# Graph layer with linear attention and routed experts on one core: expert 16's load, the low halves, the edge groups' register read, and 92 edge groups instead of 69

## What is computed

```
xn  = layernorm(x)
agg = segment_sum(xn[src], dst, 1250)              # the edges
g   = xn + relu(bn(relu(bn(((1+eps)*xn + agg) @ W1 + b1)) @ W2 + b2))
q, k = elu(xn@Wq+bq)+1, elu(xn@Wk+bk)+1 ; v = xn@Wv+bv
m   = (q (k^T v)) / (q . sum k)  per head, @ Wp + bp   # linear attention
x   = x + g + m
x   = x + experts(layernorm(x))                    # 64 experts, two per token, hash routed
```

## Time and profile before

| | us |
|---|---|
| three runs | 548.93, 550.38, 551.34 (median 550.38) |
| the profiled execution, whole | 551.58 |
| its span, first to last instruction | 549.8 |
| busy in the span: PE, DVE, ACT, POOL | 529.9, 347.8, 253.7, 90.7 |
| rows, K and edges | 9.65 to 101.9 |
| Q and edges | 101.9 to 144.8 |
| aggregation | 145.2 to 204.6 |
| dense layers and router | to 366 (their last products start at 365.9) |
| routing and first gather | 366 to 382.6 |
| 32 rounds of experts | 382.6 to 531.5 |
| the late rounds' scatter by products, output | to the end |

### The profile page before, as it was taken

How to read it: one execution, slowest core, us unless ns; L and a number is a source line. 1 busy time by engine, 2 the same in 40 slices (tenths; PEclk the granted TensorE clock), 3 DMA queues, 4 the chain that set the end, 5 groups by cost and what they waited for, 6 DMA issues and landing times.

```text
span 549.8 us, 8615 instructions
## 1 busy us (share of the span) xinstructions
PE 529.9 (96%) x2857; PEld 369.3 (67%) x2858; DVE 347.8 (63%) x985; ACT 253.7 (46%) x557; POOL 90.7 (16%) x119
## 2 busy tenths in 40 slices
PE   9899999999989999999999999996999999999997
PEld 7344444554579888799999999984545545555445
DVE  6978797777875556448886233497435534453777
ACT  4878487666445443046664211456343334333300
POOL 2304012000000000000000000004244444445310
PEclk9999999999999999999999999999899999999999
DMA  8500000000100009192008223986999999999968
GB/s 313 204 2 1 2 0 2 1 0 2 61 17 1 0 3 335 48 352 99 0 1 344 77 77 98 413 331 233 389 407 414 418 415 410 415 416 417 393 263 317
DMA packets 32426, 105.70 MB, mean 192 GB/s; under 512 B 4656, under 2 KB 10033, under 8 KB 25340
## 3 DMA queue, kind: packets, MB, share of 16 engines
q1 hardware_dynamic: 23852, 88.54, 41.5%
q0 software_dynamic: 4880, 9.78, 4.7%
q10 hardware_dynamic: 3648, 6.80, 3.4%
HBM read 93.48 MB, written 17.84 MB: 202 GB/s over the span
## 4 chain that ended last, share of the span: by engine, by line
PE 73%; DMA 9%; DVE 6%; issue 6%; ACT 2%; POOL 2%; DVEq 1%; ACTq 0%; POOLq 0%
PE PS L538 8%; PE PS L537 8%; PE PS L539 8%; PE PS L626 6%; DMA BIG<-xx_rows,TIDX 5%; PE PS L853 5%; PE PS L589 4%; PE PS L655 4%; PE PS L867 4%; PE PS L578 4%; PE PS L656 4%; PE PS L772 3%; DMA XG<-xx_rows,TIDX 3%; PE PS L615 3%; PE PS L549 2%
## 5 line engine op out<-in xcount | busy, mean ns | idle before, releaser
L537 PE MATMUL PS<-ROUND 128*128 128x416 f32 (+3 forms) x232 | 83.9, 361 | 0.0
L538 PE MATMUL PS<-ROUND 128*128 128x416 f32 (+3 forms) x232 | 83.6, 360 | 0.0
L539 PE MATMUL PS<-ROUND 128*128 128x416 f32 (+3 forms) x232 | 83.4, 359 | 0.0
L867 PE MATMUL PS<-BIG 128*64 128x512 f32 x208 | 52.9, 593 | 0.2 <-issue 0.2
L1107 DVE BATCH_NORM_STATS2 BST<-BIG 128x6 f32<-128x416 f32 (+1 forms) x36 | 20.6, 590 | 44.0 <-ACT BIG L1471 35.4
L655 PE MATMUL PS<-ROUND 128*128 128x416 f32 (+3 forms) x120 | 43.5, 363 | 2.3 <-DVE ROUND L1024 1.8
L537 PEld LDWEIGHTS PS<-ROUND 128*128 128x128 f32 (+1 forms) x232 | 43.5, 188 | 2.6
L539 PEld LDWEIGHTS PS<-ROUND 128*128 128x128 f32 (+1 forms) x232 | 43.6, 188 | 2.5
L538 PEld LDWEIGHTS PS<-ROUND 128*128 128x128 f32 (+1 forms) x232 | 43.5, 188 | 2.4
L1006 DVE TENSOR_TENSOR BIG<-PS,BIG 128x280 f32 (+17 forms) x69 | 30.6, 444 | 19.8 <-PE PS L615 16.1
L987 DVE TENSOR_SCALAR BIG<-BIG 128x180 f16<-128x180 f16 (+20 forms) x157 | 42.2, 317 | 0.0
(11 more groups left out here) (275 smaller groups left out, 974.4 us busy)
## 6 DMA issues: line engine op xcount, KB each, us to landing
BIG<-in_we SPq DMA_DIRECT2D x46, 1024.0 KB
BIG<-in_we SPq DMA_DIRECT2D x12, 512.0 KB
y_rows<-KVB SPq DMA_DIRECT2D x19, 256.0 KB
BIG<-y_rows SPq DMA_DIRECT2D x9, 512.0 KB, 8.3
EXTRA<-in_we SPq DMA_DIRECT2D x4, 1024.0 KB
XA<-in_we SPq DMA_DIRECT2D x4, 1024.0 KB
BIG<-in_wqkvp SPq DMA_DIRECT2D x3, 1024.0 KB, 10.8
XA<-in_we SPq DMA_DIRECT2D x6, 512.0 KB
```

The source lines that it names most:

```text
L537: mm(o, ah, bh, start=first, stop=False)
L538: mm(o, ah, bl, start=False, stop=False)
L539: return mm(o, al, bh, start=False, stop=last)
L867: ins = mm(PS[64 * j:64 * j + 64, b, :], HT[:, s, 128 * f2 + 64 * j:128 * f2 + 64 * j + 64], weights(2 * r + j, 1024 + 512 * f2, 512), sta ...
```

## The change

Five edits:

1. The hand-written cost in `edge_groups` counts more for a tile and for its width. The best cut has 92 groups instead of 69: of one tile 43 (6 before), of two 38 (46), of three 6 (9), of four 5 (8). `front_schedule` spreads them over the same due times as before.
2. The step `"xl"` of row tile i is due at `done + 3.4 + 2.7*i`: one in each of the first ten units of Q's products, instead of in the aggregation.
3. The register read moves from the step `"ata"` to the step `"oh"` of the same group, ahead of its one-hots, with the wait for `LOROW`.
4. `LOROW` lies in a spare part of `XG4`.
5. SyncE issues the load of expert 16 after the waits for tiles 0 to 7, ahead of the wait for tiles 8 and 9.

```diff
-            work = m * (33 + w) + 2 * (16 + w) + (best[t + m])
+            work = m * (36 + 1.6 * w) + 2 * (16 + w) + (best[t + m])
...
             if c == 0:
-                at(base + turn * i - 1.7, "xl", i)
+                at(done + 3.4 + 2.7 * i, "xl", i)
...
-        LOROW = sb("LOROW", [1, NG], I32)
+        LOROW = XG4[0:1, 418:418 + NG].bitcast(I32)
...
                     if g == 0:
                         dve.wait_ge(s_key, NKEY["key"])
                         dve.wait_ge(s_oh, 1)
+                        dve.wait_ge(sd_low, 32)
                     if g >= OHG:
                         b, use = at_of(("at", g - OHG))
                         dve.wait_ge(full[b], use)
+                    first[g] = dve.value_load(LOROW[0:1, g:g + 1], min_val=0, max_val=N - w)
...
                     g, (b, use) = step[1], at_of(("at", step[1]))
-                    if g == 0:
-                        dve.wait_ge(sd_low, 32)
                     w = GRP[g][2]
-                    first = dve.value_load(LOROW[0:1, g:g + 1], min_val=0, max_val=N - w)
...
-                    win = AT16[:, :, bass.ds(first, w)]
+                    win = AT16[:, :, bass.ds(first.pop(g), w)]
...
             for q, (i, e) in enumerate(GROUPS):
+                if q == 2:
+                    load_expert(16)
                 sp.wait_ge(sd_xx[q], 16 * (e - i))
-            load_expert(16)
             sp.wait_ge(sd_xg[1], 16)
```

More of the change, by code:

```diff
@@ L902, in link @@
                 dve.wait_ge(s_link, done[0])
+            first = {}
             KBIi, SMIi = KBI.bitcast(I32), ORD.bitcast(I32)
```

## The result

| | before | after |
|---|---|---|
| median of 10 runs each, us | 550.60 (548.93 to 552.79) | 553.24 (551.97 to 554.55) |
| ratio to before | | 1.0046, interval 1.0027 to 1.0065 |
| the profiled execution, whole / its span | 551.58 / 549.8 | 554.55 / 552.7 |
| Q's first and last product | 102.1, 144.2 | 107.3, 151.6 |
| aggregation's last product | 204.7 | 209.3 |

The change makes the kernel 2.6 us slower; 546.7 had been forecast, with 551.5 as the upper end. The loss stands complete at Q's first product (5.2 us late), grows to 7.4 at Q's last, and comes back in part: 2.8 us in the aggregation and 1.0 from the router to the first transposes.

What follows compares the result with a forecast made beforehand. The front was taken to go at TensorE's pace; -3.1 - 0.4 - 1.8 + 1.5 + 0.4 + 0 - 0.3 = -3.7 us gave 546.7 us from the 550.38 median, with an 8-in-10 range of 543.0 to 551.5.

Steps and rivals of the forecast that it cites:

- Part 1: TensorE in the front: narrower groups save 7,520 columns, -3.1 us (1.3 before Q, 1.8 in Q).
- Part 4: VectorE in Q's first nine units: 95% full, TensorE waits, +1.5 us; later reciprocals, +0.4 us.
- Part 3: Aggregation: moving low halves removes TensorE's waits, -0.4 us at its first product and -1.8 us at row tile 8.
- Part 5: VectorE's register reads: exposure and removed waits taken as equal before Q, 0 (-1.5 to +2.3 us).
- point of decision: Exposed read time for a group at which cost equals the gains, 0.21 us; above it the change loses.
- part 2: VectorE in the front: 23 more but narrower additions, 2.8 us spread over it; VectorE gets no lighter.
- the five waits that the forecast added up: TensorE's waits for VectorE's window addition in the profile before, together 3.1 us.
- Part 6: Start of the experts: expert 16's load issued 1.1 us sooner, first gather sees less of it, -0.3 us.
- The collision with the last two writes: Rival, chance 0.08: expert 16's load delays the last writes, gather up to 1.0 us later, 0.3 lost: 548.0.
- The first round at full clock: Rival, chance 0.07: a shorter wait keeps the experts' first-round clock up, gaining 1.8 us and some 0.5: 544.4.
- the reads' rival: Rival, chance 0.20: reads show and VectorE bounds Q; +8.0 us against 5.6 of gains, 552.8.
- L615's waits above 6 us: Sign in TensorE's waits for the window addition: a sum above 6 us means the reads' rival is right.

Runs made afterwards that it cites:

- e7: Kernel before with only the low halves moved into Q's units and expert 16's load issued earlier: 547.18 us, ratio 0.9943.
- e9: Changed kernel with tiles 107 to 114 in four pairs (88 groups) and the register read left at the addition: 544.63 us, ratio 0.9892.
- e12: Changed kernel (92 groups) with the register read left at the addition: 550.75 us, ratio 1.0002.
- e11: e7 with tiles 107 to 114 cut single (73 groups) and LOROW in its new place: 551.26 us, ratio 1.0012.
- e8: Changed kernel with tiles 107 to 114 in four pairs instead of eight single tiles (88 groups): 548.31 us, ratio 0.9960.
- e2: Kernel before with only the ten low halves moved among Q's products: 547.28 us, ratio 0.9945.
- e13: e12 with GpSimd's last addition of K's features waiting for the product of the fifth one-tile group: 550.45 us, ratio 1.0001.
- e5: Changed kernel with the register read behind its group's one-hots instead of ahead of them: 551.68 us, ratio 1.0028.
- e10: e8 with the register read behind its group's one-hots instead of ahead of them: 545.45 us, ratio 0.9904.
- e1: Kernel before with only expert 16's load issued ahead of the wait for the last two writes: 549.55 us, ratio 0.9984.
- e3: Kernel before with only the finer cut (92 groups) and LOROW's new place, read at the addition: 552.95 us, ratio 1.0041.
- e4: Kernel before (69 groups) with only the register read moved ahead of the one-hots and LOROW's new place: 553.21 us, ratio 1.0049.
- e14: e9 with GpSimd's last addition of K's features behind the product of the third pair: 544.91 us, ratio 0.9899.
- e6: Changed kernel with the old cut of 69 groups, read ahead of the one-hots: 547.86 us, ratio 0.9955.

## Why the forecast failed, step by step

From before to after in four steps, each kernel against its own before: edits 2 and 5 -3.0 (e7), 88 groups without the run -3.4 (e9), the run +6.1 (e12), the read moved ahead of the one-hots +2.9 (after): +2.6. Worked out from the intervals of the ratios, each of the last three steps is known to about 1.6 us either side, and the first to 1.1; e11 against e7 (+3.3) shows the run, and e8 against e9 (+4.5) the read, a second time.

**Part 1, columns: right, and they arrive.** Without the run 6,360 columns are saved, by the forecast's 0.42 ns 2.7 us; e9 is 3.4 faster than e7, each against its own before (2.6 between the medians). Before Q this cut saves 1,960 columns, 0.8 us by the same pitch; Q's first product came 1.3 sooner in the traces (100.2 for 101.5). In Q the forecast had 1.8 of gain, 1.5 of loss and 0.4 at the reciprocal, +0.1; measured from first to last product 41.7 (100.2 to 141.9) for e7's 42.3, -0.6.

**Part 4, VectorE in Q: right in size, the 1.5 too careful.** Busy time was forecast at about 29 and is 28.7 in e9, 29.6 in after. At 94% TensorE still runs full. The wait behind the first reciprocal rises from 0.67 us before to 1.19 in e9 and 1.30 in after, near the forecast's +0.4.

**Part 3, low halves: right.** -0.4 and -1.8 forecast, -0.8 and -2.0 in e2's trace. The wait of 1.78 us of the earlier trace rows is gone, and nothing else took its place.

**Part 5, reads taken at 0: the first step that failed.** They cost 2.9 us with the run (after against e12) and 4.5 without (e8 against e9). At Q's first product it is 2.0 (102.2 for 100.2), within the bound of 2.3 but at its bad end; in Q 43.6 us for 41.7, 1.9 more. What was set against it, the waits that the read had caused at 40 and 44, was not worth that: e8 has 5.0 us of TensorE's waits for the addition, nine of them, and e9 2.5 in four. The error was in weighing the read at the addition and the read at the one-hots as equal. At the addition VectorE mostly waits for TensorE anyway (in e9 8.3 of the 12.6 us of idle time there end by TensorE, 2.9 by "issue"), and the read lies inside that wait; at the one-hots nothing is waited for, so it pushes the one-hots, and with them the next product, later. The rival for this had the right place and sign, and its 552.8 is near 553.2, but not its price: with 0.29 us exposed at 21 groups in Q and at 8 before it came to 8.0, and it was 4.5 at most. In after VectorE's "issue" time ahead of one-hots is 12.0 us over 92 groups, an average of 0.13, below the 0.21 at which the forecast had set its point of decision; and e8, with the read moved and no run, is 1.9 faster than before. So the reads alone don't make the change a loss, and the rival's sum met the measured time by luck: something else, the next point, was missing from it.

**Not in the forecast at all: the run of one-tile groups.** Part 1 summed columns over stretches, and part 2 spread the 23 additions over the front. The cut doesn't spread them. One list position has five groups with nothing between them, and two banks let only two products go ahead of the additions. There a group costs a round trip of about 0.9 us and not its 0.08 us of columns. This is 6.1 us (e12 against e9), 3.3 in the old cut (e11 against e7), 4.5 with the read ahead (after against e8). The trace of before had the sign of it: three groups in that place, and 0.49 us of waiting, one of the five waits that the forecast added up. About 2.1 to 2.6 of it are waits (Q's first product in e13 and e5, against e9 and e10, all at full clock), and 1.7 the lower clock where it falls (e12 against e5). Some 2 us between these and the medians are not shown by a trace. The mean granted clock of these kernels (0.991, 0.998 in e9) points at the clock for it, but where else it fell is open.

**Part 6, load 16: right in kind, its 0.3 too small in the trace.** There it is the whole 1.1 us, the upper bound (e1); the median, 0.6, can't tell it from no change. The collision with the last two writes is not there: 3.39 us for 3.31.

**The first round at full clock: it came, and was worth little.** The rival gave 0.07 to the clock staying up, and 2.3 us to it. In the three microseconds from the first transposes on, the granted clock is 0.50 to 0.54 in the profiles of before, e3 and e4, 0.71 and 0.79 in those of e9 and e14, and 1.00 in the twelve others. So three of the four kernels without edit 5 ran this stretch at or near the lower level, and of the thirteen with it none, but two in part; over all executions the mean granted clock is 0.994 before and 0.997 in e1. This speaks for edit 5 as the cause, but with one profile for each kernel it is not shown. What the rival had wrong is the worth: from the first transposes to the end of the span it is 167.2 us before and 166.6 after, 167.5 in e1. The rounds that follow give the rest back.

**What would have shown it.** L615's waits above 6 us, which the forecast gave as the sign of the reads' rival, came (7.6), but 2.6 of them in the run; e8, without it, has 5.0. That sign couldn't tell the two.

**Still open.** Why edit 3 alone cost 3.1 us (e4) and with edits 2 and 5 only 0.7 (e6 against e7). The clock is part of it, 0.992 against 0.996; the two differences, known to about 1.4 us either side, don't exclude a common value near 2. Part of what the profiles show of it in the old cut is again the clock: in those of e4 and e6 the granted clock is 0.51 to 0.64 from 18 to 22, behind two waits of some 0.8 us, where before, e7 and e8 have 1.00. Row tile 0's first `gmm` then starts at 19.9 in e6 and 18.7 in e7, which is 1.2 of the 1.3 us between them at Q's first product. But the profile of after has two waits as long in that place (0.80 and 0.88) and a clock of 1.00, so that this comes with the moved read is not shown.

## What to carry to other kernels

When work is cut finer, count the pieces at each position of the list and not only their columns: a place where the bound engine has nothing else between two pieces is paid by the round trip through the banks, and a stall there can cost the clock as well. A register read belongs where its engine waits anyway, or behind instructions that it can hide under. A cut that a cost function has chosen is to be tried with its densest place undone; here four pairs, with the read put back, turned a loss of 0.5% into a gain of 1.1%.

## What the runs showed of the hardware

- A register read is three entries on VectorE's queue, 0.30, 0.19 and 0.02 us (the line of the read in after, min/median/max: `TENSOR_LOAD` 297/302/548 ns, `FUSED_REGOPS` 183/190/200 and `SEQ_ASSERT` 23/23/35, 92 of each).
- An f16 one-hot of VectorE stood still for the whole of a GpSimd addition of two f32 operands (1.29 us for 0.25 in e12, 1.30 in e9 at 76.05), while the window additions from PSUM beside such an addition kept their 0.51. The Trainium skill, "SBUF — State Buffer", section "SBUF: two separate sides", says that VectorE in its two-port modes and GpSimd exclude each other from a shared pair of ports for a whole instruction, whoever starts first. The durations agree, in the other direction too: in e9 GpSimd's last addition took 1.48 us for 1.27, with a one-hot of VectorE already going. That the one-hot runs in such a mode is not shown by a run here.
- The granted clock differs between executions of one kernel. Fitted over all executions, each about its own kernel's mean, 0.01 of the mean granted clock goes with about 3 us. The kernels with the run of one-tile groups have 0.991 to 0.994, e7, e9 and e14 (pairs, the read at the addition, edits 2 and 5) 0.997 to 0.998, e1 0.997, and before 0.994 to 0.995.
